# Four buffers for the loads of the scatter stage of a graph network kernel

## The reference, cut to what matters

```python
out_i = softplus(concat([x[i], edge_attr]) @ W)      # per edge, 4 heads x 64
out_j = softplus(concat([x[j], edge_attr]) @ W)      # per edge
alpha = softplus((concat([out_i, out_j]) * att).sum(-1))
alpha = segment_softmax(softplus(batchnorm(alpha)), i)
out   = segment_sum(out_j * alpha, i).mean(1) + bias
```

## Time and profile before

| what | us |
|---|---|
| median of 3 runs (7779.16 to 7788.64) | 7781.52 |
| profiled execution: its time | 7812.56 |
| profiled execution: its span | 7810.9 |
| eight indirect DMAs of the first group issued from | 657.1 |
| last indirect DMA issued at | 3706.0 |
| busy in the span: PE, DVE, ACT, POOL | 5239.3, 5449.7, 4088.4, 2029.2 |

### The profile page before, as it was taken

The page is one execution under the profiler, slowest core; times in us unless marked ns, Lnnn a source line. Parts: engine busy times, 40 slices in busy tenths (PEclk is TensorE's granted clock), DMA queues, the critical chain, the costliest instruction groups (busy, mean ns, idle before and its releaser), DMA issues. The chain is left out here.

```text
span 7810.9 us, 167729 instructions
## 1 busy us (share of the span) xinstructions
PE 5239.3 (67%) x35019; PEld 3249.2 (42%) x35020; DVE 5449.7 (70%) x28298; ACT 4088.4 (52%) x10690; POOL 2029.2 (26%) x2673
## 2 busy tenths in 40 slices
PE   2624666666666665665677777777760999996877
PEld 1212333333333333333344444444430555553877
DVE  5834665565555566654799999999988888888122
ACT  0003444444444444444677777777771889885000
POOL 0024555555554555555111111111110000000000
PEclk9956777777777777777899999999995999998878
DMA  4084444444444444444555555555540778775756
GB/s 36 2 339 167 154 154 155 153 154 149 150 153 150 152 149 150 158 151 143 173 145 144 145 145 146 144 144 144 145 120 8 214 213 221 213 213 143 318 233 265
DMA packets 932408, 1260.66 MB, mean 161 GB/s; under 512 B 294256, under 2 KB 801119, under 8 KB 910770
## 3 DMA queue, kind: packets, MB, share of 16 engines
q1 hardware_dynamic: 810402, 844.36, 38.6%
q0 software_dynamic: 88656, 333.99, 11.2%
q10 hardware_dynamic: 33216, 80.75, 2.6%
HBM read 832.90 MB, written 425.88 MB: 161 GB/s over the span
## 5 line engine op out<-in xcount | busy, mean ns | idle before, releaser
L771 POOL DMA_INDIRECT rows<-rowS,idx x1616 | 1617.2, 1001 | 1455.7 <-ACT rowS L921 961.9
L1459 DVE CUSTOM_DVE_ANT_1 junk<-bufh,attb 128x128 bf16<-128x128 f32 x7296 | 1692.0, 291 | 3.8 <-ACT bufh L1499 3.8
L1025 PE MATMUL psa<-one_c,one_s 128*128 128x392 bf16 x2352 | 668.3, 404 | 1007.6 <-ACT cnts L911 683.2
L2148 PE MATMUL psm<-msg,onem 128*128 128x260 f32 x3648 | 1009.8, 402 | 137.8 <-issue 52.1
L918 ACT ACTIVATE lgS<-preS 128x1024 f32<-128x1024 f32 x404 | 413.4, 1023 | 1223.4 <-remote 752.7
L844 DVE TENSOR_SCALAR code<-pairS,codes 128x3 f32<-128x3 f32 x784 | 202.3, 258 | 1050.7 <-remote 845.9
L2148 PEld LDWEIGHTS psm<-msg,onem 128*128 128x128 f32 x3648 | 619.5, 189 | 527.8 <-issue 473.7
L852 DVE TENSOR_SCALAR one_c<-ioc,code 128x392 bf16<-128x392 f16 x2352 | 790.4, 336 | 17.5 <-DVE code L844 0.5
L1431 POOL COPY eaC<-bufh 128x128 f32<-128x128 f32 x912 | 320.3, 351 | 1796.1 <-DMA bufh<-rows 1791.3
L1495 ACT ACTIVATE lg<-pre 128x512 f32<-128x512 f32 x912 | 544.6, 597 | 424.5 <-PE pre L1538 424.5
L2115 DVE TENSOR_TENSOR msg<-oj,alpha 128x512 f32<-128x512 f32 x912 | 630.6, 692 | 186.9 <-issue 97.6
(11 more groups left out here) (280 smaller groups left out, 8487.4 us busy)
## 6 DMA issues: line engine op xcount, KB each, us to landing
bufh<-rows SPq DMA_DIRECT2D x912, 322.0 KB, 3.0
oj<-rows SPq DMA_DIRECT2D x912, 256.0 KB
adj<-adj SPq DMA_DIRECT2D x98, 1568.0 KB, 8.0
adj<-cnts ACTq DMA_DIRECT2D x49, 1568.0 KB
eaS<-in_edge_attr_dram SPq DMA_DIRECT2D x201, 256.0 KB
low<-dlow SPq DMA_DIRECT2D x202, 252.0 KB
rows<-fill POOLq DMA_DIRECT2D x20, 1610.0 KB
rows<-fill POOLq DMA_DIRECT2D x100, 322.0 KB
```

Of the source, the lines that this page charges most:

```text
L771: eng.indirect_dma_start(out=m["rows"][h], out_offset=bass.IndirectOffsetOnAxis(ap=idx[s][:, k:k + 1], axis=0), in_=rows[s][:, k, :], in_o ...
L1025: mm = eng.matmul(psa[r][:, 0:z.GC], one_s[r][:, k, :], one_c[r][:, k, :], start=(k == 0), stop=(k == GT - 1))
L1459: ins = eng.tensor_tensor_reduce(junk[q][:, k * H + h, :, :], buf[j][:, k, :, h * D:(h + 1) * D], attb[:, :, h, :], 1.0, 0.0, ALU.mult, AL ...
L2148: mm = eng.matmul(psm[j][:, 0:C + H], one[q][:, k, :], msg[q][:, k, :], start=(k == 0), stop=(k == UT - 1))
```

## The change

The edge features, `low`, the window and each quarter's list get four buffers each, `[s]` in place of `[s % 2]` or of one, with a semaphore for each. SP issues all loads of a group together, three groups ahead, each behind the work of group t - 4 that used the buffer last; the window comes ahead of the lists. The compute engines' lists stay; only buffer and semaphore numbers change in them. `eaT` and `ohT` keep two buffers.

```diff
-        eaS = [sb(ctx, f"eaS{j}", [P, K, D], fp32) for j in range(2)]
+        eaS = [sb(ctx, f"eaS{s}", [P, K, D], fp32) for s in range(NR_BUF)]
-        low = [sb(ctx, f"low{j}", [P, K * P], bf16) for j in range(2)]
+        low = [sb(ctx, f"low{s}", [P, K * P], bf16) for s in range(NR_BUF)]
-        win = [sb(ctx, f"win{j}", [P, C], bf16) for j in range(2)]
+        win = [sb(ctx, f"win{s}", [P, C], bf16) for s in range(NR_BUF)]
-        pair = [sb(ctx, f"pairS{q}", [P, GT, 2], fp32) for q in range(GQ)]
+        pair = [[sb(ctx, f"pairS{s}_{q}", [P, GT, 2], fp32) for q in range(GQ)] for s in range(NR_BUF)]
...
             def load_ea(b, s):
-                wait(eng, turned_ready, t - 1)
-                wait(eng, ea_kept, t - 1)
+                wait(eng, turned_ready, t - 3)
+                wait(eng, ea_kept, t - 3)
...
             def load_low(b, s):
-                wait(eng, ohT_made, t - 1)
+                wait(eng, ohT_made, t - 3)
...
             def load_window(b, s):
-                wait(eng, pre_ready[1], t - 1)
+                wait(eng, pre_ready[1], t - 3)
...
             def load_pairs(b, s, q):
-                wait(eng, cols_made[q], t)
+                wait(eng, cols_made[q], t - 3)
...
+            def loads(b, s):
+                if exists(b, s):
+                    load_ea(b, s)
+                    load_low(b, s)
+                    load_window(b, s)
+                if dense(b):
+                    for q in range(GQ):
+                        load_pairs(b, s, q)
+
             def body(b, s):
-                near, two = later(b, s, 1), later(b, s, 2)
-                if exists(*two):
-                    load_ea(*two)
-                    load_low(*two)
-                more = dense(near[0])
-                if more:
-                    load_pairs(*near, 0)
-                    load_pairs(*near, 1)
-                if exists(*two):
-                    load_window(*two)
-                if more:
-                    load_pairs(*near, 2)
-                    load_pairs(*near, 3)
+                loads(*later(b, s, 3))
...
-            for s in range(2):
-                load_ea(0, s)
-                load_low(0, s)
-                load_window(0, s)
-            for q in range(GQ):
-                load_pairs(0, 0, q)
+            for s in range(3):
+                loads(0, s)
```

More of the change, by code:

```diff
@@ L631, in spread_stage @@
         cleared, v, begun = sem(ctx, "ohpad"), sem(ctx, "v_spread"), sem(ctx, "scatter_begun")
-        ea_in = [sem(ctx, f"ea_in{j}") for j in range(2)]
+        ea_in = [sem(ctx, f"ea_in{s}") for s in range(NR_BUF)]
         ea_kept = sem(ctx, "ea_kept")
         sent = [sem(ctx, f"sent{s}") for s in range(NR_BUF)]
[L635 to L638, removed]
+        low_in = [sem(ctx, f"low_in{s}") for s in range(NR_BUF)]
+        win_in = [sem(ctx, f"win_in{s}") for s in range(NR_BUF)]
+        pair_in = [[sem(ctx, f"pair_in{s}_{q}") for q in range(GQ)] for s in range(NR_BUF)]
+        cols_made, built, copied = ([sem(ctx, f"{n}{q}") for q in range(GQ)] for n in (
+            "cols_made", "built", "copied"))
         oh_ready, ohT_made, ranked, summed, idx_ready, turned_ready, evacuated = (sem(ctx, n) for n in (
@@ L663, in ea_landed @@
             short = isinstance(t, int) and t == NG - 1 and full
-            return (turns(b, s) + 1) * 16 + (16 if short else 0)
+            return (b + 1) * 16 + (16 if short else 0)
         def exists(b, s):
@@ L696, in load_ea @@
                 t = step(b, s)
[L697 to L700 removed]
+                wait(eng, turned_ready, t - 3)
+                wait(eng, ea_kept, t - 3)
+                to = eaS[s][:, :, :]
                 if isinstance(t, int) and t == NG - 1:
@@ L703, in load_ea @@
                         eng.dma_start(to[0:full, :, :], last[0:full * K, :].rearrange("(p k) d -> p k d", k=K))\
-                           .then_inc(ea_in[j], 16)
+                           .then_inc(ea_in[s], 16)
                     eng.dma_start(to[full:full + 1, 0:tail, :],
-                                  last[full * K:, :].rearrange("(p k) d -> p k d", p=1)).then_inc(ea_in[j], 16)
+                                  last[full * K:, :].rearrange("(p k) d -> p k d", p=1)).then_inc(ea_in[s], 16)
                 else:
                     a = ea_g[t] if isinstance(t, int) else ea_g[bass.ds(t, 1)].rearrange("o p k d -> (o p) k d")
-                    eng.dma_start(to, a).then_inc(ea_in[j], 16)
+                    eng.dma_start(to, a).then_inc(ea_in[s], 16)
             def load_low(b, s):
-                j = s % 2
                 t = step(b, s)
-                wait(eng, ohT_made, t - 1)
+                wait(eng, ohT_made, t - 3)
                 a = low_g[t] if isinstance(t, int) else low_g[bass.ds(t, 1)].rearrange("a o e -> (a o) e")
-                eng.dma_start(low[j][0:PW, :], a.to_broadcast([PW, P * K])).then_inc(low_in[j], 16)
+                eng.dma_start(low[s][0:PW, :], a.to_broadcast([PW, P * K])).then_inc(low_in[s], 16)
             def load_window(b, s):
-                j = s % 2
                 t = step(b, s)
                 d = eng.value_load(m["dst"][0:1, span(t * K, 1)], min_val=0, max_val=z.N - 1)
-                wait(eng, pre_ready[1], t - 1)
-                eng.dma_start(win[j][0:PW, :], m["ptab"][bass.ds(d * PARTS, PW), :]).then_inc(win_in[j], 16)
+                wait(eng, pre_ready[1], t - 3)
+                eng.dma_start(win[s][0:PW, :], m["ptab"][bass.ds(d * PARTS, PW), :]).then_inc(win_in[s], 16)
             def load_pairs(b, s, q):
@@ L727, in load_pairs @@
                 e = eng.value_load(m["startS"][0:1, span(t * GQ + q, 1)], min_val=0, max_val=NG * P * K)
-                wait(eng, cols_made[q], t)
-                eng.dma_start(pair[q][:, :, :].rearrange("p k c -> p (k c)"),
+                wait(eng, cols_made[q], t - 3)
+                eng.dma_start(pair[s][q][:, :, :].rearrange("p k c -> p (k c)"),
                               m["pairs"][bass.ds(e, GT * P), :].rearrange("(p k) c -> p (k c)", k=GT))\
-                   .then_inc(pair_in[q], 16)
-            def body(b, s):
-                near, two = later(b, s, 1), later(b, s, 2)
-                if exists(*two):
-                    load_ea(*two)
-                    load_low(*two)
-                more = dense(near[0])
-                if more:
-                    load_pairs(*near, 0)
-                    load_pairs(*near, 1)
-                if exists(*two):
-                    load_window(*two)
-                if more:
-                    load_pairs(*near, 2)
-                    load_pairs(*near, 3)
+                   .then_inc(pair_in[s][q], 16)
+            def loads(b, s):
[6 more added lines that the diff above has]
+                        load_pairs(b, s, q)
+            def body(b, s):
+                loads(*later(b, s, 3))
             def blocks(b):
@@ L799, in windows @@
                 t = step(b, s)
-                eng.wait_ge(low_in[j], (turns(b, s) + 1) * 16)
+                eng.wait_ge(low_in[s], (b + 1) * 16)
                 wait(eng, pre_ready[1], t - 1)
-                eng.tensor_scalar(ohT[j][0:PW, :, :].rearrange("p l k -> p (l k)"), low[j][0:PW, :],
+                eng.tensor_scalar(ohT[j][0:PW, :, :].rearrange("p l k -> p (l k)"), low[s][0:PW, :],
                                   m["wsc"][0:PW, span(t, 1)], None, ALU.is_equal).then_inc(ohT_made, 1)
@@ L840, in codes @@
                 r = q % 2
-                eng.wait_ge(pair_in[q], (t + 1) * 16)
+                eng.wait_ge(pair_in[s][q], (b + 1) * 16)
                 o, c = before(t, q, 2, GQ)
                 wait(eng, built[o], c)
-                eng.tensor_scalar(code[r][:, :], pair[q][:, :, 1], m["codes"][:, span(t * GQ + q, 1)], None,
+                eng.tensor_scalar(code[r][:, :], pair[s][q][:, :, 1], m["codes"][:, span(t * GQ + q, 1)], None,
                                   ALU.subtract).then_inc(code_ready, 1)
@@ L852, in column @@
                 eng.tensor_scalar(one_c[r][:, k, :], m["ioc"][:, :], code[r][:, k:k + 1], None, ALU.is_equal)
-                ins = eng.tensor_scalar(one_s[r][:, k, :], m["io128b"][:, :], pair[q][:, k, 0:1], 0.0, ALU.add,
+                ins = eng.tensor_scalar(one_s[r][:, k, :], m["io128b"][:, :], pair[s][q][:, k, 0:1], 0.0, ALU.add,
                                         ALU.is_equal)
@@ L930, in evacuate @@
                 wait(eng, sent[s], b * 16 * K)
-                eng.wait_ge(ea_in[s % 2], ea_landed(b, s))
-                eng.activation(rows[s][:, :, C:C + D], eaS[s % 2][:, :, :], ACT.Copy).then_inc(ea_kept, 1)
+                eng.wait_ge(ea_in[s], ea_landed(b, s))
+                eng.activation(rows[s][:, :, C:C + D], eaS[s][:, :, :], ACT.Copy).then_inc(ea_kept, 1)
             def body(b, s, u=None):
@@ L973, in turn @@
                 t = step(b, s)
-                eng.wait_ge(ea_in[s % 2], ea_landed(b, s))
+                eng.wait_ge(ea_in[s], ea_landed(b, s))
```

(6 more changed lines are left out.)

2 lines of the change are left out of this document (removed).

## The result

| kernel | median, us | runs |
|---|---|---|
| before | 7780.86 | 4 (7779.16 to 7788.64) |
| after | 7949.32 | 4 (7938.72 to 7962.01) |

The changed kernel takes 1.0217 of the time, 95% interval 1.0203 to 1.0232: 168 us slower. The profiled execution took 7947.37 us, its span is 7945.6 us. That is outside the range of the prediction. The profiled execution of the kernel before was 32 us above its median, so the two spans lie only 134.7 us apart, and not 168.

A forecast was written before the change was run, and what follows sets the result against it. The scatter stage was taken as bound by a circle of waits, 14.84 us per group, with PE's signals held back. 7781.5 minus 2 us of load waits, other costs nothing, gave 7780 us; 8 in 10 within 7680 to 7890.

The forecast's parts named there:

- The change touches nothing outside the stage.: All stages but the scatter stage: claimed unaffected by the change, with no term in the sum.
- Semaphores and buffers cost nothing: no instruction is added: Scatter stage: added semaphores and buffers put no instruction on PE, DVE, ACT or POOL; cost nothing.
- What it can remove are waits for loads: Scatter stage: DVE's waits for lists and `low` total 7.3 us, the most to gain directly; 2 us taken.
- SyncE's sequence: Scatter stage: SP issues window, four lists, edge features, `low` after PE's signal; steady cost nothing, at most 100 us.
- the late signal: Scatter stage: PE's signal for half 1 is held back, so exp starts 4.85 us after the product ends.
- Two engines' meeting at VectorE and GpSimd: Scatter stage: VectorE work may slow GpSimd's indirect DMA issues, 53 us at most; given nothing.
- a signal too late: Scatter stage: SP's later loads delay half 0's signal; 120 us in a quarter of groups; slower overall, chance 0.32.
- The exp of half 0 comes later than 9 us: Scatter stage: sign of the slower case, counted after the first indirect DMA, if in more than a few groups.
- signals get through earlier: Scatter stage: PE's signals pass sooner; 1.32 us less in a quarter of groups, 66 us; chance 0.30 with pairs gone.
- the long pairs: Scatter stage: eleven pairs of groups lasting 34.94 us instead of 29.68, 58 us in all; their vanishing would mean faster.
- The exp of half 1 comes before 11 us: Scatter stage: sign of the faster case, counted after the first indirect DMA, if in many groups; 11.7 us expected.
- Slower, with a chance of 0.32: Whole kernel: slower through a too-late signal or bulk loads in the scatter's way, places 7840 to 7900 us.

The follow-up runs named there:

- b_pad250: Kernel before plus 250 idle VectorE semaphore increments ahead of its half-stage work: 7074.66 us, ratio 1.0281 to the kernel before beside it.
- a_pad10: Changed kernel plus ten idle VectorE semaphore increments ahead of its half-stage work: 6883.30 us, ratio 1.0007 to the kernel before beside it.
- a_pad2: Changed kernel plus two idle VectorE instructions ahead of its half-stage work: 7802.26 us; the kernel before took 7800.83 beside it.
- b_pad122: Kernel before plus 122 idle VectorE instructions ahead of its half-stage work: 7993.52 us, half stage 2271.5 us.
- a_pad10_again: Changed kernel plus ten idle VectorE instructions, timed again where groups take 14.7 us: 7768.19 us, ratio 0.9974 to the kernel before.
- a_pad114: Changed kernel plus 114 idle VectorE instructions ahead of its half-stage work: 8212.46 us, half stage 2474.2 us.

## Why the prediction was wrong

**The step that failed** is the sentence "The change touches nothing outside the stage." It was taken as plain and had no term in the sum, no rival and no bound. With it went that the compute engines' lists stay, and the step "Semaphores and buffers cost nothing: no instruction is added". None is added, but VectorE's program has six fewer, three in each copy of the scatter stage's loop, and everything behind them moves. The profile of before doesn't show that a loop begins four places past the edge of a block; but it shows VectorE busy for 97% of the half stage, and the built programs show there a loop of 273 instructions and the six that are gone. The term that stood at nothing measured +195 us for the half stage (b_pad250: the same in a kernel without the change; a_pad10, a_pad2: gone), and 11 to 12 us that come with it in the message stage.

**"What it can remove are waits for loads", 7.3 us at most:** held. Of 7.3 us 3.8 are left, 3.5 saved at the start of the stage, where 2 were forecast.

**SyncE's sequence and "nothing" as its steady cost:** held. Window, lists, edge features, `low` come in the forecast order, edge features at 3.5 us (forecast 3.0 to 5.0, taken 3.3), GpSimd's eight issues end at 10.2 us as before, the exp of half 1 stays behind the late signal at 11.6.

**Two engines' meeting at VectorE and GpSimd, nothing:** held; GpSimd's issues take 1617 us before and 1626 after in this stage, 9 us that lie in the slack behind the last issue.

**The rival "a signal too late":** didn't occur more often than before. The exp of half 0 comes later than 9 us in 16 groups of 189, 15 before. **The rival "signals get through earlier":** the long pairs are 10 in place of 11. Short groups are 37 in place of 17 in the two profiles, but 29 in b_pad122 with the loads of before, and 16 to 18 in the executions of the changed loads at 14.9 us. The exp of half 1 comes before 11 us in 43 groups in place of 23, the sign that was named for this rival, and goes the same way: 35 in b_pad122, 21 to 25 at 14.9 us. So most of the 67 us between the profiled executions belong to the execution. Timed side by side, the change without the shift is worth 0.9974 (0.9955 to 0.9993) with late signals and 1.0007 (0.9998 to 1.0016) without them: a gain of some 16 us in the one, nothing in the other. Why it gains at all was not isolated.

**Slower, with a chance of 0.32:** came true for a reason that the text didn't have, so it is luck and no success of that number. 7780 for the stage's own effect is near the 7768.19 of a_pad10_again, which lies within 7766 to 7797; 7949 - 195 - 11 = 7743 is what the first measurement leaves for it, and a part of that distance may be the 14.7 or 14.9 us of the time of the measurement.

## What to carry to other kernels

A change of a few instructions on an engine moves every later loop of that engine. Where a loop of the bounding engine is close to a multiple of the fetched block in length, count where it begins before and after: here 273 instructions stall each pass if they begin in the last 16 places of a block of 128, which costs 5.7 us for each of 34 passes two places ahead of the edge (4.7 us twelve ahead, 6.1 us sixteen ahead). When a stage that the change doesn't touch gets slower, with the same instructions and busy times, look at the gap behind its loop's branch ("issue") and at the packets of the instruction queue in the page; a few idle instructions ahead of the loop tell at once, and mend it. Compare variants of a stage only with the later loops at a good place, or their verdicts are about placement.

## What the runs showed of the hardware

- A stall at a loop's branch, in two pieces: 3 us until the first block is there and about 2 us until the second, if the break comes two instructions in; 4.9 and 0.6 us if it comes sixteen in (a_pad114). It occurs when the loop touches four blocks of 128 instructions, not when it touches three, and it doesn't wear off: every pass has it. The Trainium skill, "Runtime: NRT & Kernel Launch", section "Instruction fetch mechanics", describes it: an engine keeps two blocks of 256 instructions, and a taken branch to a block that it no longer has waits for a DMA. The mechanism agrees with the traces; the length doesn't. By blocks of 256, b_pad122 and the first loop of a_pad114 would have had no stall, and they had one; blocks of 128 fit all twelve runs. Nor does the number of blocks: with two of 128 a loop that touches three would stall, and none did.
- The message stage takes 1121 to 1122 us in all seven profiled kernels whose half stage stalled, and 1109 to 1111 in the seven whose half stage didn't, though its own code has no long branch in any of them. What carries over wasn't found.
- TensorE's signals came late in the scatter stage on one chip and not on another. On the other chip the groups of a_pad10 follow each other without a gap (GpSimd, first issues of two groups at 1504.23 and 1515.05), and ScalarE's exp starts 0.13 us after the product of half 0 ends, 1508.54 + 0.66 = 1509.20, and 0.41 us after that of half 1, 1510.75 + 0.66 = 1511.41, in the middle of a group's eight issues, where the kernel before had 4.85 us for half 1:

```profile
1504.23 0.99 POOL L758 DMA_INDIRECT rows<-rowS,idx  x1 [0.30 <-issue]
...
1515.05 0.96 POOL L758 DMA_INDIRECT rows<-rowS,idx  x1 [0.30 <-issue]
```

```profile
1508.54 0.66 PE L1001 MATMUL preS<-win,ohT 126*128 126x256 bf16 x4
...
1510.75 0.66 PE L1001 MATMUL preS<-win,ohT 126*128 126x256 bf16 x4
```

```profile
1509.33 1.02 ACT L905 ACTIVATE lgS<-preS 128x1024 f32<-128x1024 f32 x1 [1.01 <-PE preS L1001]
...
1511.82 1.01 ACT L905 ACTIVATE lgS<-preS 128x1024 f32<-128x1024 f32 x1
```

The kernel before takes 6880 us there and 7781 to 7801 us elsewhere. What holds the signals back stays open, and a forecast of this stage holds only for a chip on which they come as late as in the profile that it was read from.
